# Identity turns on TensorE through the set-up and the first slots of a decoder layer, five normalisations moved from GpSimd to VectorE, and fewer turns ahead of the last ranks

## The reference

```python
x = x + attn(layernorm(x))                 # causal, 16 heads of 8 channels, q and k scaled by rotary factors
x = x + xattn(ctx, ctx, layernorm(x))      # one head of 128
h = layernorm(x)                           # feed-forward: 8 experts, 2 chosen per token
logits = h @ router_w.T; rw, sel = top_k(softmax(logits), 2)
y = sum over the chosen e of rw * (silu(h @ w_gate[e]) * (h @ w_up[e])) @ w_down[e]
out = x + y + sigmoid(h @ gate_w.T) * shared(h)
```

## Time and profile before

| | |
|---|---|
| median of 3 runs | 445.75 us (442.62 to 445.75) |
| profiled execution | 444.36 us |
| its span, first to last instruction | 442.6 us |
| mean granted TensorE clock in the span | 0.943 |
| PE busy | 405.7 us (92%) |
| DVE, ACT, POOL busy | 335.6, 296.8, 262.8 us |

### The profile page before, as it was taken

One profiled execution on the slowest core, in us unless ns is written; L12 is line 12 of the kernel. 1 busy time (PEld: TensorE's weight loads), 2 busy tenths in 40 slices (PEclk: granted clock), 3 DMA queues, 4 the chain that ended last, 5 costly groups with the idle time before them and its releaser, 6 DMA issues. The chain is left out here.

```text
span 442.6 us, 14454 instructions
## 1 busy us (share of the span) xinstructions
PE 405.7 (92%) x4903; PEld 311.0 (70%) x4903; DVE 335.6 (76%) x1120; ACT 296.8 (67%) x989; POOL 262.8 (59%) x318
## 2 busy tenths in 40 slices
PE   7599899999999999999999886699999999999984
PEld 6355667766767667667677655478888888888774
DVE  7433678889989899897887957494777777777477
ACT  3334588889898888898899976555556555555410
POOL 7944025172485684875636478776566666666463
PEclk9755799999999999999999999699999999999988
DMA  7603004132142231320411127131333333332296
GB/s 205 198 27 117 32 19 148 41 115 87 28 146 88 76 125 32 117 87 29 175 35 35 36 85 215 37 95 54 91 86 102 85 99 86 93 93 71 66 351 190
DMA packets 46711, 43.13 MB, mean 97 GB/s; under 512 B 6320, under 2 KB 38336, under 8 KB 46640
## 3 DMA queue, kind: packets, MB, share of 16 engines
q1 hardware_dynamic: 41150, 32.70, 23.8%
q0 software_dynamic: 4320, 8.99, 6.0%
q10 hardware_dynamic: 1170, 0.53, 0.4%
HBM read 17.26 MB, written 12.09 MB: 66 GB/s over the span
## 5 line engine op out<-in xcount | busy, mean ns | idle before, releaser
L697 POOL DMA_INDIRECT ys<-ctx_t,xload x71 | 67.9, 957 | 38.5 <-ACT ctx_t L1266 34.7
L1148 ACT ACTIVATE probs<-ps_scores 128x512 f32<-128x512 f32 x128 | 72.1, 602 | 4.7 <-PE ps_scores L830 4.7
L655 POOL DMA_INDIRECT xs<-xrow,posu x64 | 66.0, 1031 | 13.5 <-issue 11.0
L679 POOL TENSOR_SCALAR xrow<-res,mv,rs 128x128 f32<-128x128 f32 x32 | 27.1, 846 | 71.6 <-ACT rs L1196 69.8
L1012 PE MATMUL ps_scores<-wide,xe 128*128 x213 | 66.9, 423 | 0.6 <-DVE xe L1569 0.6
L1371 DVE TENSOR_REDUCE negmax<-ps_scores 128x4 f32<-128x512 f32 x64 | 41.2, 684 | 19.5 <-PE ps_scores L802 19.4
L1580 DVE COPY probs<-ps_shared 128x256 f32<-128x256 f32 x71 | 30.1, 424 | 22.2 <-PE ps_shared L1020 22.2
L1029 PE MATMUL ps_shared<-wd,probs 128*128 x284 | 43.4, 275 | 0.1
L1371 DVE TENSOR_REDUCE negmax<-s_copy 128x4 f32<-128x512 f32 x64 | 42.8, 672 | 0.9 <-ACT s_copy L1142 0.8
L1142 ACT ACTIVATE s_copy<-ps_scores 128x512 f32<-128x512 f32 x64 | 35.2, 604 | 12.1 <-PE ps_scores L802 11.3
L1261 ACT ACTIVATE vst<-ps_scores 128x256 f32<-128x256 f32 x71 | 27.2, 383 | 17.6 <-PE ps_scores L1012 17.6
(11 more groups left out here) (247 smaller groups left out, 1059.5 us busy)
## 6 DMA issues: line engine op xcount, KB each, us to landing
wide<-x_late SPq DMA_DIRECT2D x42, 256.0 KB, 2.5
xload<-xs SPq DMA_DIRECT2D x71, 66.0 KB, 1.8
wide<-ys SPq DMA_DIRECT2D x8, 512.0 KB, 8.7
ctx_t<-in_ctx SPq DMA_DIRECT2D x32, 64.0 KB, 2.0
out_x<-res SPq DMA_DIRECT2D x8, 256.0 KB, 3.1
wide<-x_late SPq DMA_DIRECT2D x6, 192.0 KB, 2.3
ys<-ctx_t,xload POOLq DMA_INDIRECT x71, 2.3
wd<-in_L_ffn_w_down SPq DMA_DIRECT2D x8, 128.0 KB, 3.4
```

Source lines behind the costliest of these rows:

```text
L655: pool.indirect_dma_start(out=xs, out_offset=bass.IndirectOffsetOnAxis(ap=posu[:, g % 2, k, u:u + 1], axis=0), in_=xrow[:, g % 2, k, u, :] ...
L697: pool.indirect_dma_start(out=ys, out_offset=bass.IndirectOffsetOnAxis(ap=xload_i[:, i % XL, C + 1:C + 2], axis=0), in_=ybuf[:, i % 4, :], ...
L1148: act.activation(probs[:, b % 2, j * HJ:(j + 1) * HJ, :].rearrange("p a t -> p (a t)"), SC[score_bank(("scores_t", b), j)][:], ACT.Exp)\
```

## The change

Turns of the identity are added: 2 become 8 behind the turned weights, 3 become 18 behind project_v(0), 14 new ones stand in turn_max(0) between the wait for its bank and the wait for the maxima, 6 in each of scores(1) to scores(4) and 8 in each of scores_t(0) to scores_t(3), both behind the wait for the four banks and written into the fourth. The turns behind router(31) become 4 instead of 10. norm_ffn of blocks 27 to 31 leaves POOL and is issued on DVE, between row_max(.., 2) and xout in the slot; the waits are the same.

```diff
         ("norm_xattn", -3, None, None),
         ("row_max", 1, 2, None),
+        ("norm_ffn", -6, None, None),
         ("xout", -5, None, None),
...
+DVE_NORMS = B - 5
...
             def norm_ffn(b):
+                if b >= DVE_NORMS:
+                    return
...
+            def free_turns(bank, n):
+
+                for _ in range(n):
+                    pe.transpose(bank[:, 0:128], ident[:], ident[:])
...
                     turned_weights()
-                    idle_turns(2)
+                    idle_turns(8)
...
                 if b == 0:
-                    idle_turns(3)
+                    idle_turns(18)
...
                 bank = w.scores_free(("scores", b))
+                if 1 <= b < 5:
+                    free_turns(bank[3], 6)
...
                 bank = w.bank_free(("turn_max", b))
+                if b == 0:
+                    free_turns(bank, 14)
                 w.ge(maxed, NJ * (b + 1))
...
                 bank = w.scores_free(("scores_t", b))
+                if b < 4:
+                    free_turns(bank[3], 8)
                 w.ge(max_placed, 16 * (b + 1))
...
                 if b == B - 1:
-                    waiting_turns(10)
+                    waiting_turns(4)
...
+            def norm_ffn(b):
+                if b < DVE_NORMS:
+                    return
+                g, u = b // GB, b % GB
+                w.ge(x2_rstd, b + 1)
+                w.ge(scattered[g % 2][u], 16 * 2 * (g // 2))
+                dve.tensor_scalar(xrow[:, g % 2, 0, u, 0:C], res[:, b, :], mv3[:, 0:1], rs3[:, 0:1], ALU.subtract, ALU.mult)\
+                    .then_inc(xn3_ready, 1)
```

More of the change, by code:

```diff
@@ L1546, in weight @@
                     .then_inc(wgu_split, 1)
-            w.run("DVE", dict(norm_x_stats=norm_x_stats, turn_x=turn_x, project=project, row_max=row_max, tall_sums=tall_sums, attn_out=attn_out, norm_xattn=norm_xattn, xscores=xscores,
+            w.run("DVE", dict(norm_x_stats=norm_x_stats, turn_x=turn_x, project=project, row_max=row_max, tall_sums=tall_sums, attn_out=attn_out, norm_xattn=norm_xattn, norm_ffn=norm_ffn, xscores=xscores,
                        turn_xprobs=turn_xprobs, xout=xout, router=router, route=route, ranks=ranks, split=split, weight=weight))
```

## The result

The changed kernel takes 452.49 us (median, 451.93 to 454.69), where the kernel before took 445.75 beside it (442.62 to 446.27): ratio 1.0182, 95% interval 1.0149 to 1.0216. It is slower by 6.7 us, and the forecast was 440.7 with a range to 446. The profiled execution took 452.1 us with a span of 450.3.

| | before | after | difference |
|---|---|---|---|
| scores(0) | 16.83 | 16.68 | -0.15 |
| scores(1) | 23.42 | 23.90 | +0.48 |
| scores(5) | 57.44 | 60.58 | +3.14 |
| xout(27) on DVE | 261.65 | 264.69 | +3.04 |
| ranks(7) on TensorE | 287.47 | 293.12 | +5.65 |

What follows compares the result with a forecast made beforehand. Early attention slots were taken as bound by the score-bank ring at TensorE's low clock, the end by one block's chain across engines. 444.36 - 4.4 (front) + 0.7 (parts 4 and 5) = 440.7 us, range 436.0 to 446.0.

Steps and rivals of the forecast that it cites:

- Part 1: Set-up: 21 more identity turns, 2.3 us, lie wholly in the DMA wait before scores(0), cost nothing and keep the clock full.
- Part 2: Slot 0: 14 turns ahead of turn_max(0) overrun the maxima by 0.4 us; slot 0 becomes some 6.0 us (-0.6).
- the first rival: Clock falls once in slot 0; 14 turns take 3.0 us, part of slot 1 stays cold: 443.7 us; chance 0.25.
- Part 3: Slots 1 to 4: exposed turns cost 0.64 and 0.85 us per slot, but full clock gains 2.3, 0.7, 0.2, 0.6.
- the rival given 0.06: Score-bank ring, slots 1 to 4: turns do not hold the clock, all exposed, 14.3 us slower: 458.7; chance 0.06.
- the warm ring: Score-bank cycle at full clock in the early slots: 2.45 and 3.51 us, with turns 7.45 us per slot.
- Part 4: End of attention slots: last five feed-forward norms on DVE wait behind younger blocks' work; net +1.3 us up to router(31).
- Part 5: Ahead of ranks(7): four turns instead of ten bring ranks 1.28 us earlier, of which only 0.6 counts.

Runs made afterwards that it cites:

- the first bank: All added turns, norms on POOL, slots' turns waiting for and writing the first freed score bank instead of the fourth: ratio 0.9799 to the kernel before.
- the early norms: Kernel before with only the five norms on DVE, placed behind attn_out instead of behind row_max: 445.85 us, ratio 0.9997.
- set-up turns, early norms and four turns: Kernel before plus set-up turns, 14 ahead of turn_max(0), norms on DVE behind attn_out, four turns behind router(31): ratios 0.9631, 0.970, 0.9716, 0.9752.
- the first series: The first four experiments, up to the norms on DVE behind attn_out, run beside the kernel before at 446.01 us.
- the later series: Four further series of experiments, in which the kernel before took 492.22, 486.66, 492.34 and 485.58 us.

## Why the prediction was wrong

**Part 1, right.** The set-up turns lie in the wait for the DMA, 0.81 us of it is left for the 0.8 on record, and the clock is full at scores(0).

**Part 2, its size off, as the first rival had it.** The clock fell in slot 0, at 19.2 us, while TensorE idled 0.98 us for the bank. The fourteen turns took 3.22 us and overran the maxima (ready at 20.64) by 1.95 us, for 0.4 on record, and slot 0 7.22 instead of 6.0 (before 6.59). The sum also left out the six turns of scores(1), which stand at the end of slot 0: it counts three sets of six where the change has four. They took 0.75 us of the 7.22. In the one profile of these turns in which the clock did not fall in slot 0, it took 5.74 us with them, and the overrun was 0.5 us. The clock was full again at 22.6 us, before slot 1 began, so the rival's second half (part of slot 1 cold) did not come.

**Part 3, the step that failed.** Its sentence was that the value stands near the warm rows "because the turns are dense and the fall came while TensorE stood idle". The turns stand behind the very waits in which TensorE stands idle, so they are dense where it is busy anyway and leave the idle time as it was. I had noted that they are behind the wait for the banks, used this for their price and not for their effect on the clock. TensorE was at the low level in 7.2 of the 10.58 us of slot 3 and 5.3 of the 9.21 of slot 4, against 7.45 and 6.8 us on record for the two slots: the rival given 0.06 was the right mechanism there. Its 458.7 had all four slots low. For slots 1 and 2, at the full clock, the sum was near: 8.83 and 8.06 against 8.6 and 7.45. The price of the turns themselves was right, 6.3 us for 6.0. That the place of the turns matters for the clock rests on the two profiles at the first bank, which have no fall in slots 2 to 4. Why one program has its clock low for 3.4 us in one profile and for 13.6 in others, the runs do not show.

A second fault lies in what the gain was set against. I weighed the warm ring with turns (forecast 30.3 us from scores(1) to scores(5)) against the cold one of before (34.0) and never against the ring with the set-up turns and none in the slots, which needs 25.9 to 28.8. The gain of the front comes from the turns ahead of slot 1 alone, which leave scores(5) 5.6 us earlier. Even if the forecast had come true, scores(5) would have started at 53.1 us, later than without the slots' turns (51.8).

The forecast of -4.4 was not out of reach for this front: in the one profile with the short form scores(5) starts at 54.71, 2.7 us earlier than before. The four executions of the result, 451.93 to 454.69 us, are none of them near that.

**Part 4, the mechanism right, its size off.** The moved norm is held by its place in DVE's order, and TensorE waits for it, as written. But the lags add up: to 4.46 us at xout(30), not 2.0. I gave each block 1.0 us of which 0.6 counts; the first two cost 1.20 and 0.95, the third 2.31, with TensorE at the low level from 272 us on, where the kernel before is at the full one until 279. The gains for blocks 30 and 31 came as written in sign (-0.44 and -0.42 against -0.1 and -0.3). Net +3.6 instead of +1.3, of which up to 1.6 can be the clock's phase, as said with the early norms.

**Part 5, right.** From xout(31) to ranks(7) the changed kernel takes 5.09 us, that with the norms alone 6.36: 1.27 us, for 1.28 on record. hidden(0) then starts 2.63 us behind ranks(7) instead of 1.92 and gives 0.7 of it back, for 0.7 on record.

**The rule on transpose mode.** "TensorE: Matmul & The Clock Gate", Part 4, in the Trainium skill says that transposes do not engage the full clock. The runs go against it: in all fifteen profiles with the added set-up turns scores(0) runs at the full level, its burst 0.67 us, and in all five without them at the low one, 1.12 us. The kernel got slower without that rule being right, by the turns' own time and by the low stretches that they did not prevent.

The sum: 7.5 us of the miss in the front (+3.1 for -4.4; of this 5.5 in slots 3 and 4, 1.2 in slot 0, 0.8 in slots 1 and 2), 3.0 in the tail up to the tile loop (+3.7 for +0.7), 1.0 behind it.

Open: how fast set-up turns, early norms and four turns are in a series like the first; why the low level lasts 31 us in the front before and 3.4 us at a time once the clock is full at scores(0); and what the 14 turns ahead of the maximum are worth without the 21. The fastest kernel measured in the first series is the one with the turns ahead of slot 1 alone, 439.67 us.

## What to carry to other kernels

An idle turn is free only in front of the wait that makes the engine idle, and needs a bank that is free before that wait ends; behind the wait it costs its full time (6.3 us for 56 of them here, at like clock), and in four of five profiles of the changed front the clock was lower with them than without. Holding the clock is not yet a gain: the turns at the first bank held it, and the front was no shorter. When a part of a change is to pay by making something else fast, price that effect without the part as well: here 21 turns in a DMA wait and 14 ahead of a maximum had the whole gain, and the 56 beside them took 9 us back. An instruction moved to a faster engine should be placed by what stands ahead of it there: the same five instructions cost 0 or 4 us by their row in the list.

## What the hardware showed unexpectedly

**The same kernel, several fronts.** With one program the clock was low for 3.4 us or for twice 6.8 in slots 3 and 4, and scores(1) to scores(5) 4.5 us longer. Without turns in the slots it was low for 3.4, 6.8 or 10.1 us in eight profiles, and the stretch 25.9, 27.4 or 28.8 us. The front of before is no exception: 34.0 us in three profiles, 31.6 in that of the early norms, in which scores(0) starts at 20.75 instead of 16.8. A single profile does not tell what such a change does to the clock.

**Series that are 9 to 10% longer.** In the later series, on four chips, one of them the chip of the first series, instructions take as long as before (the 128x256 copy of the tile loop 424 and 423 ns), but VectorE and ScalarE pause with no wait that the profile names. The waits of ACT over the span, first the kernel before, in which this is the one such entry:

```profile
ACT woT L1109 <- issue: 1.5, 1, 1.5
```

and the kernel with four turns ahead of ranks(7) as its only edit, in a series in which the kernel before took 492.22 us:

```profile
ACT xe L1256 <- issue: 14.7, 26, 1.1
ACT probs L1221 <- remote: 13.2, 2, 10.8
...
ACT vst L1261 <- issue: 4.8, 12, 1.1
```

In the tile loop such a pause turns every fifth or so of the iterations from 1.47 us into 2 to 3 us, and TensorE waits for DVE once. The timeline of TensorE in the change without its slots' turns, one such iteration:

```profile
373.80 0.94 PE L1023 MATMUL ps_scores<-wide,xe 128*128 x3
375.74 0.44 PE L1031 MATMUL ps_shared<-ident,vst 128*128 128x128 f32 x2 [1.00 <-DVE vst L1594]
```

Bytes and packets of the DMA queues are the same in both. In the kernel with four turns as its only edit the extra time lies from scores(5) to xout(27) (14.5 us), from ranks(7) to the first expert tile (12.1) and in the tile loop (18.1). What causes the pauses the traces don't tell. They leave the front up to 60 us as it was, which is why its starts could be compared, and they hide effects of a few us near the end of the slots.
